# ScalarE's order in an attention head, the first batch's split and mask terms on other engines, and expert routing by groups

## The reference

```python
# layer 0: 256 Runge-Kutta steps of an oscillator network driven by x, then a feed-forward net
x = x + ffn0(oscillator(cond, cond, x, coupling, bias), W1, W2, W3)
# layer 1: attention over channels, B=8 batches, x[b] is (C=256, T=512), 16 heads of 16 channels
Q, K, V = proj(Wq), proj(Wk), proj(Wv)
att = einsum('bhqd,bhkd->bhqk', Q, K) / sqrt(16) + b[0]
att = att * m + (1.0 - m) * -1e30            # m = mask[b, k]
att = softmax(att); y = einsum('bhqk,bhkd->bhqd', att, V)
# experts: E=8, two per token, F=256
scores = y @ router_w
weights, idx = top_k(softmax(scores), 2); weights /= weights.sum()
x = x + sum over the two experts of weight * down(silu(gate(y)) * up(y))
```

## Time and profile before

| what | us |
|---|---|
| median of the runs | 3033.29 |
| the profiled execution | 3030.47 |
| its span | 3028.6 |
| TensorE busy, matmul | 2534.4 (84%) |
| VectorE busy | 2531.1 (84%) |
| ScalarE busy | 1214.7 (40%) |
| GpSimd busy | 1348.8 (45%) |
| mean granted TensorE clock | 0.962 |

### The profile page before, as it was taken

The page is one execution under the profiler, slowest core; times in us unless marked ns, Lnnn a source line. Parts: engine busy times, 40 slices in busy tenths (PEclk is TensorE's granted clock), DMA queues, the critical chain, the costliest instruction groups (busy, mean ns, idle before and its releaser), DMA issues. The chain is left out here.

```text
span 3028.6 us, 112026 instructions
## 1 busy us (share of the span) xinstructions
PE 2534.4 (84%) x41104; PEld 1773.0 (59%) x41104; DVE 2531.1 (84%) x11914; ACT 1214.7 (40%) x4102; POOL 1348.8 (45%) x3951
## 2 busy tenths in 40 slices
PE   4478888888888888888888778888888876999999
PEld 4356666666666666666666546666666652444444
DVE  7989999999999999999998459999999976445544
ACT  3343333333333333333333348888888850000000
POOL 6846566656565656655655224434343344000000
PEclk6599999999999999999999889999999998999999
DMA  4100000000000000000000341111111110000000
GB/s 183 43 20 3 10 10 10 10 3 10 10 10 3 10 10 10 10 3 10 10 10 3 129 136 47 32 30 47 47 47 47 33 71 0 15 13 28 0 28 14
DMA packets 43893, 88.57 MB, mean 29 GB/s; under 512 B 7168, under 2 KB 23808, under 8 KB 41600
## 3 DMA queue, kind: packets, MB, share of 16 engines
q1 hardware_dynamic: 36336, 63.11, 6.6%
q10 hardware_dynamic: 4752, 10.49, 0.9%
q0 software_dynamic: 2304, 8.39, 0.9%
HBM read 65.18 MB, written 16.78 MB: 27 GB/s over the span
## 5 line engine op out<-in xcount | busy, mean ns | idle before, releaser
L228 PE MATMUL rest<-Tl,CW 128*128 128x56 f16 x16384 | 618.9, 190 | 313.5 <-DVE Tl L494 313.5
L228 PEld LDWEIGHTS rest<-Tl,CW 128*128 128x128 f16 x16384 | 503.3, 97 | 560.5 <-DVE Tl L494 556.6
L347 ACT ACTIVATE Tf<-X 128x32 f32<-128x32 f32 x768 | 176.0, 229 | 778.5 <-DVE X L538 778.5
L1082 ACT ACTIVATE Pr<-negL,nM 128x512 f32<-128x512 f32 x512 | 357.9, 729 | 16.8 <-DVE nM L1112 16.8
L1112 DVE CUSTOM_DVE_ANT_0 negL<-Lps,negC 128x512 f32<-128x512 f32 x512 | 339.6, 682 | 21.2 <-PE Lps L1020 18.0
L1030 PE MATMUL Tps<-idS,Pr 128*128 128x128 f32 x2048 | 282.9, 282 | 87.2 <-ACT Pr L1082 86.9
L1132 DVE TENSOR_TENSOR PT<-Tps,PT 128x512 f16<-128x512 f32 x512 | 348.2, 681 | 7.3 <-ACT PT L1089 2.5
L625 POOL TENSOR_TENSOR G<-X,Dr 128x32 f32<-128x32 f32 x768 | 205.9, 268 | 301.7 <-DVE X L499 274.2
L1089 ACT ACTIVATE PT<-Tps 128x512 f16<-128x512 f32 x512 | 292.3, 597 | 98.1 <-PE Tps L1030 98.0
L1030 PEld LDWEIGHTS Tps<-idS,Pr 128*128 128x128 f32 x2048 | 222.0, 142 | 177.5 <-ACT Pr L1082 148.3
L217 PE MATMUL main<-Th,CW 128*128 128x56 f16 x8224 | 264.1, 189 | 10.2 <-DVE CW L450 10.2
(11 more groups left out here) (133 smaller groups left out, 5147.1 us busy)
## 6 DMA issues: line engine op xcount, KB each, us to landing
stage<-w_up SPq DMA_DIRECT2D x8, 1024.0 KB, 4.8
qk<-qkp ACTq DMA_DIRECT2D x32, 256.0 KB, 2.4
QR<-qk SPq DMA_DIRECT2D x128, 64.0 KB, 2.2
KR<-qk SPq DMA_DIRECT2D x128, 64.0 KB, 2.4
wstage<-moe_up POOLq DMA_DIRECT2D x16, 512.0 KB, 5.4
W2m<-w_down SPq DMA_DIRECT2D x1, 4096.0 KB, 13.4
stage<-x_tb SPq DMA_DIRECT2D x16, 256.0 KB, 2.7
x<-stage SPq DMA_DIRECT2D x16, 256.0 KB, 2.1
```

Of the source, the lines that this page charges most:

```text
L228: last = pe.matmul(rest[:, m], CW[:, 0, k, m * P:(m + 1) * P], Tl[:, k:k + 1, :].to_broadcast([P, REP, B]), start=(m == 0 and k == 0), sto ...
L1082: act.activation(Pr[:, h % 2, qt, :], negL[:, qt, :], ACT.Exp, bias=nM[:, h % 4, qt:qt + 1], scale=-1.0).then_inc(s_exp, 1)
```

## The change

It has four parts. In attention, ScalarE's step takes the exponential of a query tile ahead of the roundings that go with it. In projections, the first batch's input is rounded by ScalarE and its remainder made by VectorE, and GpSimd starts with the second. The mask terms of the first batch are made by VectorE in the projections block, from the masks loaded there and a `b0S` loaded there by SyncE; attention's SyncE starts with mask row 1 and loads the row of batch b + 2 behind Q and K of b + 1. In experts, TensorE starts with two `gate_up` blocks and makes the scores behind them; VectorE routes one group of four tiles at a time, behind the two hidden blocks with which the group begins; ScalarE takes each group's exponential behind two tanh; the loop over groups is written out.

```diff
@@ projections
             def _(sp):
                 sp.dma_start(wst[:], w_qk).then_inc(in_w, 16)
+                sp.dma_start(b0S[:], b0.partition_broadcast(P)).then_inc(in_b0, 16)
...
-                with pool.Fori(0, B // 2) as bb:
-                    for j in range(2):
...
+                pool.wait_ge(x_lo, 3)
+                split_input(0, 1)
+                with pool.Fori(1, B // 2) as bb:
+                    split_input(bb, 0)
+                    split_input(bb, 1)
...
                 act.dma_start(masks[:], mask.partition_broadcast(P)).then_inc(in_m, 16)
+                act.wait_ge(in_x[0], 16)
+                act.activation(xh[:, 0, 0].rearrange("p c n -> p (c n)"), xb[:, 0].rearrange("p c n -> p (c n)"),
+                               ACT.Copy).then_inc(x_hi, 1)
...
+                dve.wait_ge(x_hi, 1)
+                dve.tensor_tensor(xh[:, 0, 1], xb[:, 0], xh[:, 0, 0], ALU.subtract).then_inc(x_lo, 1)
+                dve.wait_ge(in_m, 16)
+                dve.wait_ge(in_b0, 16)
+                dve.tensor_scalar(kf[:, 0], masks[:, 0], -1.0, 1.0, ALU.mult, ALU.add).then_inc(first_mask, 1)
+                dve.tensor_scalar(kf[:, 1], masks[:, 0], b0S[:, 0:1], None, ALU.mult).then_inc(first_mask, 1)
+                dve.wait_ge(first_mask, 2)
+                dve.scalar_tensor_tensor(negC[:], kf[:, 0], NEG, kf[:, 1], ALU.mult, ALU.subtract).then_inc(first_mask, 1)
+                dve.wait_ge(first_mask, 3)
                 with dve.Fori(0, B // 2) as bb:
@@ attention
-            sp.dma_start(b0S[:], b0.partition_broadcast(P)).then_inc(in_id, 16)
-            sp.dma_start(mrow[:], mask[0].partition_broadcast(P)).then_inc(in_mask, 16)
+            sp.dma_start(mrow[:], mask[1].partition_broadcast(P)).then_inc(in_mask, 16)
...
-            with sp.Fori(0, B - 1) as b:
-                sp.wait_ge(negc_t, 3 * b + 3)
-                sp.dma_start(mrow[:], mask[b + 1].partition_broadcast(P)).then_inc(in_mask, 16)
+            with sp.Fori(0, B - 2) as b:
                 for half in range(2):
 
                     sp.wait_ge(s_L, b * 64 + 32 * (half + 1))
                     load_qk(sp, b + 1, half)
+                sp.wait_ge(negc_t, 3 * b + 6)
+                sp.dma_start(mrow[:], mask[b + 2].partition_broadcast(P)).then_inc(in_mask, 16)
...
-            pool.sem_inc(negc_ok, 1)
-            mask_terms(0)
+            pool.sem_inc(negc_ok, 2)
+            pool.sem_inc(negc_t, 3)
...
                 for qt, kcs in ((0, (0, 1)), (1, (2,)), (2, (3,)), (3, ())):
+                    if exists(b, h, 0):
+                        exps(b, h, qt)
                     for kc in kcs:
                         if exists(b, h, 1):
                             transposed_high(*before(b, h, 1), kc)
-                    if exists(b, h, 0):
-                        exps(b, h, qt)
@@ experts, TensorE
-            pe.wait_ge(r_lo, 1)
...
+            for g in range(NG):
                 gate_up(g, 0, 0)
                 gate_up(g, 0, 1)
+                if g == 0:
+                    scores()
                 with pe.Fori(1, E) as e:
@@ experts, ScalarE
+            for g in range(NG):
+                for fc in range(FC):
+                    gate_tanh(g, 0, fc)
+                group = slice(g * TT, (g + 1) * TT)
+                act.wait_ge(dif_ok, g + 1)
+                act.activation(ex[:, group], dif[:, group], ACT.Exp, scale=1 / WS).then_inc(ex_ok, 1)
+                with act.Fori(1, E) as e:
@@ experts, VectorE
-            route()
-            with dve.Fori(0, NG) as g:
+            for g in range(NG):
                 hidden(g, 0, 0)
                 hidden(g, 0, 1)
+                route(g)
                 dve.wait_ge(acc_in, (g + 1) * TT * 16)
-                dve.sem_inc(halt, 1)
```

More of the change, by code:

```diff
@@ L694, in attention @@
         V = sb("V", [P, B, DC, NH, VW], F16)
+        negC = sb("negC", [P, D])
+        b0S = sb("b0S", [P, 1])
         with ExitStack() as c1:
@@ L989, in step @@
                 real = exists(b, h, 0)
-                if h == 0 and real:
+                if h == 0 and real and not (isinstance(b, int) and b == 0):
                     mask_sum(b)
@@ L1013, in _ @@
                 pe.sem_inc(s, AHEAD)
-            pe.wait_ge(in_id, 32)
+            pe.wait_ge(in_id, 16)
             def scores(b, h, qt):
@@ L1259, in down, with scores @@
                     last.then_inc(d_mm, 1)
[L1262 to L1270, removed]
+            def scores():
+                pe.wait_ge(r_lo, 1)
+                for tt in range(NT):
+                    k = 0
+                    for wp, Yp in ((0, YH), (1, YH), (0, YL)):
+                        for qt in range(DC):
+                            last = pe.matmul(dp[0][:, tt * E:(tt + 1) * E], Yp[:, tt // 2, qt, (tt % 2) * P:(tt % 2 + 1) * P],
+                                             rw[:, wp, qt, :], start=(k == 0), stop=(k == 3 * DC - 1))
+                            k += 1
+                last.then_inc(sc_mm, 1)
+            for g in range(NG):
                 gate_up(g, 0, 0)
                 gate_up(g, 0, 1)
+                if g == 0:
+                    scores()
                 with pe.Fori(1, E) as e:
@@ L1303, in _, with step, route @@
             dve.sem_inc(hid_ok, FC)
[L1305 to L1317, removed]
+            steps = [0]
+            def step(ins):
+                ins.then_inc(own, 1)
+                steps[0] += 1
+                dve.wait_ge(own, steps[0])
+            def route(g):
+                if g == 0:
+                    dve.wait_ge(sc_mm, 1)
+                    step(dve.tensor_copy(sc[:].rearrange("p t e -> p (t e)"), dp[0][:, 0:NT * E]))
+                    dve.sem_inc(folded, TT)
+                tiles, group = range(g * TT, (g + 1) * TT), slice(g * TT, (g + 1) * TT)
+                for tt in tiles:
                     last = dve.max(top[:, tt], sc[:, tt])
                 step(last)
-                for tt in range(NT):
+                for tt in tiles:
                     last = dve.max_index(idx[:, tt], top[:, tt], sc[:, tt])
+                dve.tensor_tensor(dif[:, group], top[:, group, 1], top[:, group, 0], ALU.subtract).then_inc(dif_ok, 1)
                 step(last)
-                dve.tensor_tensor(dif[:], top[:, :, 1], top[:, :, 0], ALU.subtract).then_inc(dif_ok, 1)
-                step(dve.tensor_copy(idf[:], idx[:, :, 0:2]))
-                dve.wait_ge(ex_ok, 1)
-                step(dve.tensor_scalar(den[:], ex[:], WS, WS, ALU.mult, ALU.add))
-                step(dve.reciprocal(wt[:, 0], den[:]))
-                step(dve.tensor_tensor(wt[:, 1], wt[:, 0], ex[:], ALU.mult))
-                for tt in range(NT):
+                step(dve.tensor_copy(idf[:, group], idx[:, group, 0:2]))
+                dve.wait_ge(ex_ok, g + 1)
+                step(dve.tensor_scalar(den[:, group], ex[:, group], WS, WS, ALU.mult, ALU.add))
+                step(dve.reciprocal(wt[:, 0, group], den[:, group]))
+                step(dve.tensor_tensor(wt[:, 1, group], wt[:, 0, group], ex[:, group], ALU.mult))
+                for tt in tiles:
                     last = dve.tensor_scalar(c1[:, tt], io[:], idf[:, tt, 0:1], wt[:, 0, tt:tt + 1], ALU.is_equal, ALU.mult)
```

39 lines of the change are left out of this document (18 added, 21 removed).

## The result

The changed kernel takes 3098.48 us (median; 3097.0 to 3099.52), the kernel before 3033.55 on the same chip: a ratio of 1.0215, interval 1.0198 to 1.0233. It is slower by 65 us. Forecast were 3096, in 3075 to 3118.

A forecast was written before the change was run, and what follows sets the result against it. ScalarE's ring was taken to set attention's 5.24 us head, TensorE to bound experts but for one hole. Attention +79.3, experts -15, projections -1.4, mask terms -0.5 gave +62.4: 3092.9 profiled, forecast 3096 us, range 3075 to 3118.

The forecast's parts named there:

- three hand-overs: Attention: A0 to E0, E0 to H0, H0 to B0 sum to 1.98 us, making a head 5.87, 0.63 more.
- B0: Attention: VectorE's first residual of the head before, forecast to start 1.98 us after A0 instead of 1.35.
- H0: Attention: ScalarE's first rounding for the head before; B0 waits for it, forecast 0.62 us behind E0.
- E0: Attention: ScalarE's first exponential of the new head, forecast 0.73 us after A0 and now ahead of H0.
- A1: Attention: VectorE's second negate-and-max of a head, 0.61 us after A0 in the steady head; B0 comes next.
- The hole: Experts: TensorE's standstill before gate-and-up, until routing and a hidden block are done, forecast at 13 us, not 26.
- the other case: Projections: the 1.75 us pause before the memset is not GpSimd's doing, so nothing is gained; end +0.3.
- VectorE freed: Attention rival: E0 merely fills ScalarE's hole, head goes to 5.10 us, total 2998; chance 0.08.
- A0: Attention: VectorE's first negate-and-max of a head, forecast 5.87 us from one head to the next.
- The clock: Attention rival: TensorE's clock falls as its load drops; up to 3250 us, likelier 3130; chance 0.05.
- the orders weigh the same: Attention rival: ScalarE's change is neutral and only experts gain, 3016 us; chance 0.02.
- Routing's escape from GpSimd: Experts rival: routing's small operations pass GpSimd's long one, TensorE doesn't stop, 3079 us; chance 0.05.

The follow-up runs named there:

- e1: Kernel before with only ScalarE's new order, the exponential of a query tile ahead of its roundings: 3114.67 us, 1.0278 to before.
- e6: Kernel after with ScalarE's first rounding put back ahead of the first exponential, the rest still alternating: 3016.73 us, 0.9954 to before.
- e4: Kernel after with b0 loaded on ScalarE's queue and GpSimd's first expert-weight loads held until the first negate-and-max: 3093.95 us, 1.0206 to before.
- e7: Kernel after with early negate-and-max, short scaling, GpSimd's weight loads held back, memset moved, first gate-and-up released earlier: 2991.03 us, 0.9867 to before.
- e8: e7 with ScalarE's old order in the first head of each batch only: 2985.5 us, 0.9846 to before.
- e5: Kernel after with VectorE's first negate-and-max of the next head, within a batch, ahead of its reciprocal and last remainder: 3006.65 us, 0.9919 to before.
- e2: Kernel after with ScalarE's old order in attention put back: 3016.4 us, 0.9955 to before.
- e3: Kernel after with GpSimd's scaling of the down weights in 8 pieces of 2 slices: 3085.59 us, 1.0178 to before.

## Why the prediction was right, and where it was not

**The head.** The step that carried the forecast, three hand-overs of 0.73, 0.62 and 0.63 where VectorE had 1.35, was right: 0.72, 0.63 and 0.61, B0 at 1.96 (forecast 1.98), 3.89 behind it, head 5.85 (5.87). Attention came out at +80.9 against +79.3, and the closeness is in part luck: the forecast gave every head the 0.63, while steady heads grew by 0.61 and the 27 short ones of the kernel before by about 0.75. e1 shows that the swap does it alone, e6 that H0 behind E0 is the place. B0 stands 1.35 behind A1, 0.74 more than the pitch of 0.61, as forecast with 0.75; the list shows 0.66 as idle, since the row maximum of A1 is read out for 0.08 in between. TensorE's share was forecast to drop to 77% and dropped to 82%: its busy time a head, whose ends are modelled, did not stay at 4.55 us.

**Experts.** The hole was forecast at 13 us and is 11.70. The prediction's own times do not give 13: TensorE stops at 2493.5 + 15.5 = 2509.0 and restarts at 2523.4, which is 14.4. Nor did 14 of 16 tiles lie behind 2510.49 in the kernel before: VectorE's timeline has the pairs of 10 tiles there, those of four more are listed before it. The forecast for the new order did not use that count, but the 4.86 us with two tiles and 1.3 for two more; from the scaling's end to the restart it had 12.8 and it is 11.8. A routing operation of about 15 us beside the scaling is there with 13.91. Routing of groups 1 to 3 costs nothing (TensorE's waits for hidden blocks there are 8.5 us in four, 8.8 before). No table load shows: the tanh behind the exponential starts 0.03 us after its end, so none of the switches that the prediction weighed is there. The term is -18.84 instead of -15. Restart after the hole is 48.01 us into the stage, 48.76 before, with three blocks of 5.18, 15.54 us of work, done that were not: -16.3, close to the forecast. A further 1.69 is one slow down-projection that the profiled execution of before has and that of after has not; 0.9 stays open. One more step was wrong and did not matter: TensorE did not start with SyncE's first load but 2.5 us later, since its buffers were released behind VectorE's wait for the router weights.

**Start of attention.** Forecast -0.5, measured +2.7. I counted the issue that SyncE lost and the terms that GpSimd lost, and did not ask what stood behind those terms on GpSimd's queue: its own weight loads. e4 shows the mechanism and its price, 3.2 us; with these loads held back the start is 11.04, which is 0.46 below before, the -0.5 of the forecast.

**Projections.** Forecast -1.4, measured +1.54 with the weights landing 1.53 later, so nothing without that. From ScalarE's first operation to TensorE's it is 6.61 us before and 6.68 after. The step that failed is that the 1.75 us in front of the memset were GpSimd's doing; the prediction named the other case and gave it the end of +0.3. The pause is the memset's own, and with the memset out of the way (e7, e8) the distance is 5.66 and 4.55.

By the marks the terms were off by +1.6 (attention), -3.8 (experts), +3.2 (start) and +2.9 (projections), and the oscillator added 2.1: the sum is +68.4 where +62.4 was forecast. The experts' miss hid part of the others. That the median of 3098.48 lies only 2.5 us above the 3096 is luck as well: the forecast added 2.8 us for the distance of the profiled execution of before from its median, and the kernel after has no such distance (3098.81 profiled). From profiled to profiled execution the forecast was 3092.9, 5.9 us low.

**The rivals.** "VectorE freed" described a gain that this change does not have: with the early A0 as well, the heads do take 5.11 (e5). The clock stayed at 0.99. That the orders weigh the same is ruled out by e1 and e2. Routing's escape from GpSimd, forecast at 3079, came about only when the scaling was cut (e3, 3085.59).

## What to carry to other kernels

When two engines pass work to and fro in a fixed order, an operation moved up on one of them can cost time if what it waits for does not come up on the other too; add up the hand-overs to the operation that is next due, and do it apart for the steps of a loop in which a neighbour is missing. When work is taken off a queue, look at what is queued behind it and starts early in its place. Keep small operations on VectorE away from long ones on GpSimd, or cut the long ones.

## What was not expected of the hardware

- **A pause in front of a strided memset.** VectorE's memset of the ones of V (512 elements a partition, strided) shows 1.74 to 1.76 us of idle time in front of it, put down to issue, in all ten kernels, and it moves with the memset. Whether the stride has to do with it is open.
- **The clock behind short waits.** TensorE waits 2.13 or 2.21 us at the end of each of the four expert groups. Behind it the block of 24 matmuls took 5.35 us in 30 of 40 places and 7.00 to 7.04 in the other ten, with no order that I could see: none in the kernel after, e2 and e5, one in before, e1, e4 and e6, two in e3, e7 and e8. The two cases in the stretches, e8 from 2591 and the kernel after from 2708 us (the clock is the number behind GpSimd's busy time):

```profile
2591.00:2598.20 7.20, 7.00 (x25) 2.89 (x26) 2.39 (x4) 0.00 (x0) 0.00 (x0) 0.76 0.19 73
```

```profile
2708.00:2714.00 6.00, 5.68 (x27) 2.62 (x28) 2.80 (x5) 0.00 (x0) 0.00 (x0) 1.00 0.23 87
```

- **The clock behind small matmuls.** The 192 router matmuls of 8 columns are listed as keeping TensorE busy for the whole stretch, at a granted clock of 1.00. Right behind them it is 0.55, near the lower level, 1.2 GHz, and the next block starts with 3.49 us for 8 matmuls that take 1.89 otherwise. The stretches with the scores and behind them, in the kernel after:

```profile
2576.60:2581.20 4.60, 4.60 (x189) 4.60 (x188) 3.02 (x3) 0.00 (x0) 4.08 (x5) 1.00 0.22 81
2581.40:2585.00 3.60, 3.60 (x13) 1.28 (x11) 3.32 (x14) 0.00 (x0) 3.34 (x3) 0.55 0.00 0
```
